# Thirty-eight products that nobody reads, in the attention's tail and the first score step of a one-core decoder block

## The chip, the cores and the metric

The kernel runs on one core of a Trainium2 chip. The metric is the device time of one execution in microseconds. Three executions of the kernel before took 869.7, 869.7 and 870.72 us; the median is 869.7 us. Lower is better.

## The reference

The block has three sublayers on x of 8 batches, 128 tokens and 256 features, each with a layer norm ahead and a residual add behind:

```
x = x + delta_rule_attention(layernorm(x))   # 16 heads, state 128 x 256 a head, causal convolutions
x = x + cross_attention(layernorm(x), ctx)   # 16 heads of 8 features, 256 rows against 256
x = x + experts(layernorm(x))                # shared + 8 experts, two of them weighted in
```

The cross attention treats the 256 features of a batch as 256 rows of 128 tokens. For each batch and head it computes

```
dot  = einsum('bhdt,bhds->bhts', q, k) / sqrt(8)
amap = softmax(mask * dot - (1 - mask) * 1e6) * mask
out  = einsum('bhts,bhds->bhdt', amap, v)
```

## The kernel before, in words

Each engine has its instructions written out in order by hand, and semaphores tie the engines together. PE's stream (the kernel's last long function) has these parts.

First come 32 steps of the delta-rule attention (STEPS = 32: 16 heads in two halves of four batches). Their pieces, such as `proj_`, `grams`, `c_t1`, `y0`, `y1` and `outp`, are interleaved. Behind the last full step comes a tail in which the pieces of the last steps, `s30` to `s32`, stand among the projections of the cross attention: `k_proj` (keys, L2210 and L2211), `v_proj` (values, L2222) and `q_proj` (queries, L2233 and L2234). `outp` (L2079) makes the last sublayer output, which DVE adds to x (L1479). DVE then takes the moments of the new x (L1345, L1348) and normalizes it (L1354).

Then PE has a row of waits on semaphores, for everything of the attention, and goes on to the cross attention. It has 64 units: a unit is two heads' 256 x 256 scores of one batch, so that a batch has 8. For unit n `top_scores(n)` (L2352) makes the scores in PSUM, DVE takes their maxima (L1693), and POOL splits the negative maxima of four units into two f16 parts (L755, L757, L759: `mrow`). `turn_max` (L2364) transposes these onto the query stack's rows and DVE adds them (L1685), so that `energies(n)` (L2377) makes scores with the maximum already taken off. ACT takes the exponential (L1193, `et`), and `values` (L2394) multiplies by the values into the bank `avb`. `swap_den` (L2404) exchanges halves of the denominators once a batch. DVE's L1616 stacks a query projection's high and low parts; ACT's L1129 makes the high part.

`batch_step(w)` is one of eight steps over the batches. It holds eight `top_scores`, eight `energies` (six units behind), the `values` of up to four pairs, two `turn_max` and up to four halves of `q_proj`, in a fixed order. Scores and energies share three pairs of PSUM banks in rotation, so that `top_scores(3)` waits for the first maximum. Step 0 has no `values` and only two `energies` at its end. Behind the eight steps come the rest of the cross attention and the experts.

`t.matmul(out, stationary, moving)` is the form of a product. `ident16` is a 128 x 128 identity in f16, `kst` the stacked keys in f16, and `avb` is bank 6 of PSUM, which holds nothing that is still needed at the places of the change.

Of the kernel before, what the change touches and what calls it, by code (L numbers as in the profile page):

```python
# [105 lines left out]
def need(eng, sem, value):  # L106

    if isinstance(value, int) and value <= 0:
        return
    eng.wait_ge(sem, value)  # L110
# [13 lines left out]
def build(nc, d, out):  # L124
    with ExitStack() as whole:
# [3 lines left out]
        def sb(name, shape, dt, ctx=whole):  # L129
            return ctx.enter_context(nc.sbuf_tensor(name, shape, dt))  # L130
# [10 lines left out]
        ident16 = sb("ident16", [P, P], F16)  # L141
# [16 lines left out]
        kst = sb("kst", [P, B, 4, H], F16)  # L158
# [184 lines left out]
        avb, misc = psum[:, 6, :], psum[:, 7, :]  # L343
# [12 lines left out]
        def pair_of(kind, n):  # L356
            return pairs[place[kind, n] % 3]
# [1495 lines left out]
        def _(pe):  # L1853
            t = nc.tensor
# [342 lines left out]
            def k_proj(bb, hh):  # L2197

                pe.wait_ge(ctx_masked, bb + 1)
                if bb == 0:  # L2200
                    pe.wait_ge(mask_ready, 1)
                    pe.wait_ge(bias_ready, 1)
                    pe.wait_ge(z_sb[hh], STEPS - 1)
                elif bb == NK:
                    pe.wait_ge(z_sb[hh], STEPS)
                else:
                    pe.wait_ge(k_stack[hh], bb)
                for g2 in range(2):
                    o = ubank[hh][:, g2 * H:(g2 + 1) * H]
                    t.matmul(o, wks[:, 2 * hh + g2], ctxs[:, bb], start=True, stop=False)  # L2210
                    mm = t.matmul(o, bias5[:, 1, 2 * hh + g2], mask5[:, bb], start=False, stop=True)  # L2211
                mm.then_inc(k_psum[hh], 1)

            def v_proj(i):
# [7 lines left out]
                    mm = t.matmul(ebank[i % 2][:, n * P:(n + 1) * P], ctxs[:, 2 * i + n // 2, n % 2 * P:(n % 2 + 1) * P], wvt[:], start=True, stop=True)  # L2222
                mm.then_inc(v_psum[i % 2], 1)

            def q_proj(h, g2):
                b, hh = h // 2, h % 2
                if g2 == 0:
                    pe.wait_ge(x_masked, b + 1)
                    need(pe, q_stack, h)
                    if h >= 3:  # L2230
                        pe.wait_ge(q_full, h - 2)
                o = misc[:, g2 * H:(g2 + 1) * H]
                t.matmul(o, wqs[:, 2 * hh + g2], xm[:, b], start=True, stop=False)  # L2233
                mm = t.matmul(o, bias5[0:4, 0, 2 * hh + g2], mask5[0:4, b], start=False, stop=True)  # L2234
                if g2 == 1:
                    mm.then_inc(q_psum, 1)
# [75 lines left out]
            k_proj(6, 1)  # L2312
            pe.wait_ge(added, STEPS * 2 - 2)
            q_proj(0, 0)
            q_proj(0, 1)
            k_proj(7, 0)
            s32.y1()
            k_proj(7, 1)
            q_proj(1, 0)
            q_proj(1, 1)  # L2320
            s32.outp(0)
            s32.outp(1)


            pe.wait_ge(z_sb[0], STEPS)
# [11 lines left out]
            def pair_free(kind, n):  # L2337
                user = freed(kind, n)
                if user is not None:
                    pe.wait_ge(max_done if user[0] == "max" else e_done, user[1] + 1)  # L2340

            def top_scores(n):
                if not 0 <= n < UNITS:
                    return
                h, g2, rp = n // 4, n // 2 % 2, n % 2
                b, gq = h // 2, h % 2 * 2 + g2
                pe.wait_ge(q_stack, h + 1)
                pair_free("max", n)
                for tt in range(2):
                    for rr in range(2):  # L2350
                        ps = slice(32 * (2 * rp + rr), 32 * (2 * rp + rr) + 32)
                        mm = t.matmul(pair_of("max", n)[:, rr, tt * H:(tt + 1) * H], qst[ps, h % 4, g2, tt * P:(tt + 1) * P], kst[ps, b, gq, :], start=True, stop=True)  # L2352
                mm.then_inc(max_psum, 1)

            def turn_max(h):
                if not 0 <= h < 2 * B:
                    return
                pe.wait_ge(max_split, 3 * h + 3)
                need(pe, q_stack, min(h + 3, 2 * B))
                need(pe, q_full, h)  # L2360
                for g2 in range(2):
                    for tt in range(2):
                        o = g2 * H + tt * P
                        mm = t.transpose(misc.bitcast(F16)[:, o:o + P], mrow[:, h % 2, tt, g2].rearrange("p r n -> p (r n)"), ident16[:])  # L2364
                mm.then_inc(row_psum, 1)

            def energies(n):
                if not 0 <= n < UNITS:
                    return
                h, g2, rp = n // 4, n // 2 % 2, n % 2  # L2370
                b, gq = h // 2, h % 2 * 2 + g2
                pe.wait_ge(q_full, h + 1)
                pair_free("exp", n)
                for st in range(2):
                    for rr in range(2):
                        ps = slice(32 * (2 * rp + rr), 32 * (2 * rp + rr) + 32)
                        mm = t.matmul(pair_of("exp", n)[:, rr, st * H:(st + 1) * H], kst[ps, b, gq, st * P:(st + 1) * P], qst[ps, h % 4, g2, :], start=True, stop=True)  # L2377
                mm.then_inc(e_psum, 1)

            def values(gn, st):  # L2380
                if not 0 <= gn < 4 * B:
                    return
                b, gq = gn // 4, gn % 4
                if st == 0:
                    pe.wait_ge(e_done, 2 * gn + 2)
                    if gq == 0:
                        pe.wait_ge(v_wide, 2 * b + 2)
                        need(pe, den_ln, b)
                        if b == 0:
                            pe.wait_ge(late_set, 4)  # L2390
                half_ = gq // 2 * H
                for r in range(4):
                    ps = slice(32 * r, 32 * r + 32)
                    mm = t.matmul(avb[ps, half_:half_ + H], vz[:, b % 2, st, r, 32 * gq:32 * gq + 32], et[:, gn % 4, r, st],  # L2394
                                  start=(gq == 0 and st == 0), stop=(gq % 2 == 1 and st == 1), skip_group_check=True)
                if st == 1:
                    mm.then_inc(o_psum, 1)

            def swap_den(b):
                if not 0 <= b < B:  # L2400
                    return
                pe.wait_ge(den_sb, b + 1)
                pe.wait_ge(num_sb, b + 1)
                t.matmul(avb[:, 0:H], swap[:], den[:], start=True, stop=True).then_inc(swap_psum, 1)  # L2404

            def batch_step(w):
                values(4 * w - 5, 0)
                top_scores(8 * w)
                values(4 * w - 5, 1)
                energies(8 * w - 6)  # L2410
                turn_max(2 * w - 1)
                top_scores(8 * w + 1)
                energies(8 * w - 5)
                if 2 <= 2 * w + 2 < 2 * B:
                    q_proj(2 * w + 2, 0)
                top_scores(8 * w + 2)
                swap_den(w - 2)
                if 2 <= 2 * w + 2 < 2 * B:
                    q_proj(2 * w + 2, 1)
                energies(8 * w - 4)  # L2420
                top_scores(8 * w + 3)
                values(4 * w - 4, 0)
                energies(8 * w - 3)
                values(4 * w - 4, 1)
                top_scores(8 * w + 4)
                values(4 * w - 3, 0)
                energies(8 * w - 2)
                values(4 * w - 3, 1)
                turn_max(2 * w)
                top_scores(8 * w + 5)  # L2430
                energies(8 * w - 1)
                values(4 * w - 2, 0)
                top_scores(8 * w + 6)
                if 2 <= 2 * w + 3 < 2 * B:
                    q_proj(2 * w + 3, 0)
                energies(8 * w)
                top_scores(8 * w + 7)
                if 2 <= 2 * w + 3 < 2 * B:
                    q_proj(2 * w + 3, 1)
                values(4 * w - 2, 1)  # L2440
                energies(8 * w + 1)

            for w in range(B):
                batch_step(w)
# [230 lines left out]
```

## Time and profile before

| | |
|---|---|
| median of three runs | 869.7 us (869.7 to 870.72) |
| the profiled execution | 870.83 us, span 869.0 us |
| PE busy, share of the span | 804.5 us, 93% |
| DVE, ACT, POOL busy | 712.8, 657.7, 619.0 us |
| mean granted TensorE clock | 0.963 |
| chain that ended last | PE 84%, POOL 4%, DVE 4% |

The span is the time from the first to the last instruction; the execution's own time is 1.8 us longer. The page's second part cuts the span into 40 slices of 21.7 us. The digit of an engine is its busy share in tenths, and PEclk is the TensorE clock that was granted, in tenths of full speed; slice 32 begins at 673.5 us. In the table by stretches the columns are start and end, length, and for each engine the busy time with the number of instructions, then the granted clock, the share of DMA and GB/s. In a timeline a row is: start, time from the first start to the last end, engine, line, operation, tiles, shapes and count, and in brackets the idle time before it with what ended it. PE's products overlap, so that the distance between two starts is the price of one, and the duration is longer.

### The profile page before, as it was taken

What the parts mean: (1) busy time and instruction counts of PE and PEld (TensorE: products, weight loads), DVE (VectorE), ACT (ScalarE), POOL (GpSimd) and SP (SyncE); (2) the same over time, 40 slices, a digit from 0 to 9 for tenths busy, and PEclk for the clock granted to TensorE, in tenths of its full rate; (3) what the DMA queues carried; (4) which work ended last, traced back from release to release, by engine and by line L of the source; (5) the groups of instructions that cost most, each with busy time, mean ns of one, the idle gap of its engine ahead of it and who ended that gap; (6) DMA issues with size and microseconds to landing.
All of it is one profiled execution on the core that took longest, in us unless ns stands there. A gap on an engine that the chain in (4) does not pass through costs nothing.

```text
span 869.0 us, 22776 instructions
## 1 busy us (share of the span) xinstructions
PE 804.5 (93%) x7798; PEld 551.9 (64%) x7834; DVE 712.8 (82%) x1202; ACT 657.7 (76%) x1036; POOL 619.0 (71%) x749
## 2 busy tenths in 40 slices
PE   3589999999999999999999999999999699999987
PEld 2257777777777777777777777777775233433554
DVE  6788888898888888888889888899677858996634
ACT  3688888888888888888888888888733347876633
POOL 4879979898898988989898898986650214342248
PEclk9999999999999999999999999999999559995999
DMA  8301000000100001000000100000000700000051
GB/s 225 114 2 38 25 14 26 14 26 12 36 24 12 24 12 36 15 21 24 12 24 12 36 24 12 0 1 2 2 2 0 122 6 2 2 2 1 2 134 49
DMA packets 32032, 24.94 MB, mean 29 GB/s; under 512 B 3310, under 2 KB 29614, under 8 KB 31851
## 3 DMA queue, kind: packets, MB, share of 16 engines
q1 hardware_dynamic: 29227, 19.75, 8.1%
q0 software_dynamic: 2752, 4.49, 2.5%
q8 instruction: 33, 0.54, 0.3%
q14 instruction: 20, 0.16, 0.1%
HBM read 25.85 MB, written 1.06 MB: 31 GB/s over the span
## 4 chain that ended last, share of the span: by engine, by line
PE 84%; POOL 4%; DVE 4%; issue 3%; ACT 2%; DMA 1%; SPq 1%; POOLq 0%; DVEq 0%; ACTq 0%
PE psum L1904 18%; PE psum L1975 7%; PE psum L2079 6%; PE psum L2394 4%; PE psum L2047 4%; PE psum L2058 3%; PE psum L2003 3%; PE psum L1922 3%; PE psum L1921 3%; PE psum L1920 3%; PE psum L2233 2%; PE psum L1996 2%; PE psum L1962 2%; PE psum L2006 2%; PE psum L2210 2%
## 5 line engine op out<-in xcount | busy, mean ns | idle before, releaser
L1461 DVE SCALAR_TENSOR_TENSOR y<-psum,cwh,y 128x508 f32<-128x508 f32 (+2 forms) x384 | 281.9, 741 | 11.1 <-ACT y L938 2.1
L558 POOL TENSOR_TENSOR ct<-lm,levels 128x256 f16<-128x256 f32 x224 | 151.0, 704 | 8.1 <-DVE lm L1472 8.1
L544 POOL TENSOR_TENSOR sql<-sq,sqh 128x1024 f16<-128x1024 f32 x32 | 68.4, 2137 | 58.7 <-ACT sqh L995 38.8
L938 ACT ACTIVATE y<-psum,cwh 128x512 f32<-128x512 f32 x128 | 99.2, 775 | 3.2 <-PE psum L1904 3.1
L1193 ACT ACTIVATE et<-psum 128x1024 f32<-128x1024 f32 x64 | 64.6, 1023 | 34.2 <-PE psum L2377 34.1
L1904 PE MATMUL psum<-xth,whi 128*128 128x512 f16 x256 | 77.0, 383 | 10.7 <-DVE y L1461 7.9
L1693 DVE TENSOR_REDUCE mx<-psum 128x4 f32<-128x1024 f32 x64 | 75.8, 1218 | 13.4 <-PE psum L2352 13.1
L1904 PE MATMUL psum<-xth,wlo 128*128 128x512 f16 x256 | 77.1, 383 | 0.0
L1904 PE MATMUL psum<-xtl,whi 128*128 128x512 f16 x256 | 77.0, 383 | 0.0
L1429 DVE TENSOR_TENSOR ux<-ux,psum 128x512 f16<-128x512 f16 x96 | 65.8, 686 | 6.6 <-PE psum L2006 6.0
L1975 PE MATMUL psum<-kq 128*128 128x256 f32 x256 | 70.0, 397 | 0.0
L1920 PE MATMUL psum<-woh,vth 128*128 128x256 f16 x256 | 69.8, 273 | 0.0
L1921 PE MATMUL psum<-wol,vth 128*128 128x256 f16 x256 | 69.8, 273 | 0.0
L1922 PE MATMUL psum<-woh,vtl 128*128 128x256 f16 x256 | 69.8, 273 | 0.0
L755 POOL TENSOR_SCALAR mxs<-mx 128x16 f32<-128x16 f32 x16 | 4.0, 252 | 90.9 <-DVE mx L1693 90.9
L531 POOL TENSOR_TENSOR vtl<-vt,vth 128x1024 f16<-128x1024 f32 x32 | 68.4, 2138 | 0.1
L931 ACT ACTIVATE zz<-psum 128x512 f32<-128x512 f32 x64 | 38.2, 597 | 35.2 <-PE psum L1922 35.1
L2079 PE MATMUL psum<-zz,pt 128*128 128x256 f32 x256 | 63.1, 389 | 0.0
L2003 PE MATMUL psum<-t1z,ux 128*128 128x64 f16 x768 | 54.1, 193 | 8.7 <-ACT t1z L922 8.7
L525 POOL TENSOR_TENSOR vth<-vt,zero 128x1024 f16<-128x1024 f32 x32 | 60.6, 1894 | 0.0
L1996 PEld LDWEIGHTS psum<-ux,ct 128*128 128x128 f16 x768 | 42.7, 98 | 24.5 <-DVE ux L1429 2.6
L2003 PEld LDWEIGHTS psum<-t1z,ux 128*128 128x128 f16 x768 | 40.3, 97 | 24.6 <-ACT t1z L922 12.1
(239 smaller groups left out, 2293.3 us busy)
## 6 DMA issues: line engine op xcount, KB each, us to landing
wraw<-in_L_attn_Wv SPq DMA_DIRECT2D x32, 128.0 KB, 2.4
wo<-in_L_attn_Wo SPq DMA_DIRECT2D x16, 256.0 KB, 2.8
wraw<-in_L_attn_Wk SPq DMA_DIRECT2D x16, 128.0 KB, 2.2
wraw<-in_L_attn_Wq SPq DMA_DIRECT2D x16, 128.0 KB, 2.3
x<-in_x SPq DMA_DIRECT2D x8, 128.0 KB, 3.8
maskrow<-in_mask_row POOLq DMA_DIRECT2D x1, 1024.0 KB, 5.0
ctxs<-in_ctx SPq DMA_DIRECT2D x1, 1024.0 KB, 7.1
wide<-comb_mem SPq DMA_DIRECT2D x4, 256.0 KB, 5.1
```

Source lines behind the costliest of these rows:

```text
L531: g.tensor_tensor(lo, f, hi, ALU.subtract).then_inc(v_split, 1)
L558: g.tensor_tensor(dst, src, pick.unsqueeze(1).to_broadcast([P, NB, T // (2 * m), m]), ALU.mult).then_inc(masked[l], 1)
L938: s.activation(y[:, n], ubank[n % 2].rearrange("p (j t) -> p j t", j=NB), ACT.Identity, scale=cwh[:, (a.c // 2) % 2, n, TAPS - 1:TAPS], bi ...
L1461: v.scalar_tensor_tensor(out=y[:, n, :, sh:], in0=u[:, :, 0:T - sh], scalar=cwh[:, (a.c // 2) % 2, n, TAPS - 1 - sh:TAPS - sh], in1=y[:, n ...
L1693: v.tensor_reduce(mx[:, h % 2, g2, 2 * rp:2 * rp + 2].rearrange("p r a -> p (r a)"), pair_of("max", n).rearrange("p r (a s) -> p (r a) s", ...
L1904: mm = t.matmul(ubank[n % 2], w_[:, hr, n, ch, :], x_[:, ch, cols], start=(m == 0), stop=(m == len(ops) - 1))
L1920: t.matmul(o, vth[:, r, vc, toks], woh[:, hr, vc, :], start=(vc == 0), stop=False)
L1921: t.matmul(o, vth[:, r, vc, toks], wol[:, hr, vc, :], start=False, stop=False)
L1922: mm = t.matmul(o, vtl[:, r, vc, toks], woh[:, hr, vc, :], start=False, stop=(vc == 1))
L1975: mm = t.matmul(ebank[hf][:, jj * 256:(jj + 1) * 256], kq[:, r, j, 0, :], kq[:, r, j].rearrange("p a t -> p (a t)"), start=True, stop=True)
L2003: mm = t.matmul(half(dst[:, 256 + j * 64:256 + (j + 1) * 64], m), turned(st.c % 2, 0, j), first_half(t1z[:, level - 1, j * T:(j + 1) * T], ...
L2079: mm = t.matmul(c_banks(c)[hf][:, jj * H:(jj + 1) * H], pt[:, j], zz[:, c.c % 2, j], start=True, stop=True)
```

## The change

A new function `keep_busy(n)` makes n products of the identity with 512 columns of the key stack into `avb`. No semaphore is raised by them and none is waited for, and no engine reads what they write; the first `values` begins the bank anew. Fourteen stand in the tail: 3, 2, 2 and 3 between `q_proj(0, 1)` and `q_proj(1, 0)`, and 4 behind the last `outp`, ahead of the row of waits. Twenty-four stand in step 0 of the cross attention, three behind each of its eight `top_scores`. Nothing else differs: the opening of the two kernels is the same.

```diff
+            def keep_busy(n):
+                for _ in range(n):
+                    t.matmul(avb, ident16[:], kst[:, 0, 0:2].rearrange("p g n -> p (g n)"), start=True, stop=True)
+
             pe.wait_ge(added, STEPS * 2 - 2)
             q_proj(0, 0)
             q_proj(0, 1)
+            keep_busy(3)
             k_proj(7, 0)
+            keep_busy(2)
             s32.y1()
+            keep_busy(2)
             k_proj(7, 1)
+            keep_busy(3)
             q_proj(1, 0)
             q_proj(1, 1)
             s32.outp(0)
             s32.outp(1)
+            keep_busy(4)
...
             def batch_step(w):
                 values(4 * w - 5, 0)
                 top_scores(8 * w)
+                if w == 0:
+                    keep_busy(3)
                 values(4 * w - 5, 1)
                 energies(8 * w - 6)
                 turn_max(2 * w - 1)
                 top_scores(8 * w + 1)
+                if w == 0:
+                    keep_busy(3)
...
```

The same two lines stand behind the other six `top_scores` of the step.

PE's order from the last key projection to the first scores, before (L2210 and L2211 keys, L2233 and L2234 queries, L2079 `outp`, L2352 scores):

```order
L2210 MATMUL psum<-ctxs,wks 128x256
L2211 MATMUL psum<-mask,bias 128x256
L2233 MATMUL psum<-xm,wqs 128x256
L2234 MATMUL psum<-mask,bias 128x256
L2233 MATMUL psum<-xm,wqs 128x256
L2234 MATMUL psum<-mask,bias 128x256
L2079 MATMUL psum<-zz,pt 128x256 x4
L2352 MATMUL psum<-kst,qst 128x256 x8
```

The same place now (L2227 is `keep_busy`, L2237 and L2238 the queries, L2361 the scores):

```order
L2210 MATMUL psum<-ctxs,wks 128x256
L2211 MATMUL psum<-mask,bias 128x256
L2227 MATMUL psum<-kst,ident 128x512 x3
L2237 MATMUL psum<-xm,wqs 128x256
L2238 MATMUL psum<-mask,bias 128x256
L2237 MATMUL psum<-xm,wqs 128x256
L2238 MATMUL psum<-mask,bias 128x256
L2079 MATMUL psum<-zz,pt 128x256 x4
L2227 MATMUL psum<-kst,ident 128x512 x4
L2361 MATMUL psum<-kst,qst 128x256 x4
L2227 MATMUL psum<-kst,ident 128x512 x3
```

Three products now stand ahead of the last query projection and so ahead of `outp`, four behind it, and the first two units' scores are apart.

PE's order around the first `turn_max` (L2364), before: the scores of units 3 and 4, the transposes, the scores of units 5 and 6, half a projection, the first energies (L2377) and the scores of unit 7:

```order
L2352 MATMUL psum<-kst,qst 128x256 x8
L2364 MATMUL psum<-ident,mrow 128x128 x4
L2352 MATMUL psum<-kst,qst 128x256 x8
L2233 MATMUL psum<-xm,wqs 128x256
L2234 MATMUL psum<-mask,bias 128x256
L2377 MATMUL psum<-qst,kst 128x256 x4
L2352 MATMUL psum<-kst,qst 128x256 x4
```

The same place now, from the scores of unit 4 (L2373 the transposes, L2386 the energies):

```order
L2361 MATMUL psum<-kst,qst 128x256 x4
L2227 MATMUL psum<-kst,ident 128x512 x3
L2373 MATMUL psum<-ident,mrow 128x128 x4
L2361 MATMUL psum<-kst,qst 128x256 x4
L2227 MATMUL psum<-kst,ident 128x512 x3
L2361 MATMUL psum<-kst,qst 128x256 x4
L2227 MATMUL psum<-kst,ident 128x512 x3
L2237 MATMUL psum<-xm,wqs 128x256
L2238 MATMUL psum<-mask,bias 128x256
L2386 MATMUL psum<-qst,kst 128x256 x4
L2361 MATMUL psum<-kst,qst 128x256 x4
L2227 MATMUL psum<-kst,ident 128x512 x3
```

Three products stand ahead of the transposes, and six between them and the projection and energies that follow.

## Rows read from the trace of the kernel before

**Rows 1.** The page's slices: the granted clock.

```profile
PEclk9999999999999999999999999999999559995999
```

**Rows 2.** Busy time by stretch: tail, first step, half clock, a full step, the end.

```profile
660.00:670.00 10.00, 10.00 (x55) 5.89 (x53) 7.30 (x15) 3.56 (x7) 1.58 (x2) 1.00 0.00 0
670.00:690.00 20.00, 12.68 (x84) 5.95 (x83) 17.65 (x28) 5.14 (x8) 4.74 (x10) 0.69 0.43 80
700.00:710.00 10.00, 10.00 (x70) 3.37 (x70) 4.96 (x6) 4.03 (x5) 1.42 (x4) 0.50 0.00 0
728.60:741.80 13.20, 13.17 (x151) 5.40 (x151) 12.18 (x15) 10.37 (x15) 5.22 (x13) 1.00 0.01 2
784.00:804.00 20.00, 19.75 (x164) 6.54 (x162) 12.98 (x27) 12.46 (x17) 5.76 (x14) 0.50 0.00 1
```

**Rows 3.** The same by single microseconds, where the clock falls, rises and falls.

```profile
677.00:678.00 1.00, 0.00 (x0) 0.00 (x0) 1.00 (x2) 0.22 (x1) 0.00 (x0) 0.88 0.41 122
...
718.00:719.00 1.00, 1.00 (x16) 0.23 (x12) 1.00 (x2) 0.98 (x2) 0.03 (x1) 0.64 0.00 0
...
783.00:784.00 1.00, 0.81 (x9) 0.29 (x8) 1.00 (x2) 0.66 (x2) 0.00 (x0) 0.78 0.00 0
```

**Rows 4.** Timeline of PE, from the last output product to the first transposes.

```profile
670.78 1.99 PE L2079 MATMUL psum<-zz,pt 128*128 128x256 f32 x8
674.28 0.41 PE L2352 MATMUL psum<-kst,qst 32*128 32x256 f16 x8 [1.51 <-DVE x L1479]
674.62 0.70 PE L2233 MATMUL psum<-xm,wqs 128*128 128x256 f32 x2
...
675.68 0.70 PE L2233 MATMUL psum<-xm,wqs 128*128 128x256 f32 x2
...
678.48 0.61 PE L2352 MATMUL psum<-kst,qst 32*128 32x256 f16 x4 [1.89 <-DVE mx L1693]
...
682.89 0.61 PE L2364 MATMUL psum<-ident,mrow 128*128 128x128 f16 x4 [2.67 <-POOL mrow L759]
```

**Rows 5.** Timeline of DVE in the same stretch.

```profile
672.18 1.32 DVE L1479 TENSOR_TENSOR x<-x,psum 128x512 f32<-128x512 f32 x2
...
677.12 4.61 DVE L1693 TENSOR_REDUCE mx<-psum 128x4 f32<-128x1024 f32 x4
...
684.08 3.49 DVE L1693 TENSOR_REDUCE mx<-psum 128x4 f32<-128x1024 f32 x3
```

**Rows 6.** Timeline of PE: first query projections of steps 1 to 4, and one swap.

```profile
690.77 1.22 PE L2233 MATMUL psum<-xm,wqs 128*128 128x256 f32 x2
...
712.83 1.22 PE L2233 MATMUL psum<-xm,wqs 128*128 128x256 f32 x2
...
728.60 0.67 PE L2233 MATMUL psum<-xm,wqs 128*128 128x256 f32 x2
...
729.63 0.70 PE L2404 MATMUL psum<-den,swap 128*128 128x256 f32 x2
730.16 0.59 PE L2233 MATMUL psum<-xm,wqs 128*128 128x256 f32 x2
...
741.79 0.67 PE L2233 MATMUL psum<-xm,wqs 128*128 128x256 f32 x2
```

**Rows 7.** Timeline of PE in the opening: L1904, products of 512 columns.

```profile
25.44 0.59 PE L1904 MATMUL psum<-xth,whi 128*128 128x512 f16 x2 [1.08 <-DVE y L1461]
25.87 0.59 PE L1904 MATMUL psum<-xtl,whi 128*128 128x512 f16 x2
...
29.66 1.01 PE L1904 MATMUL psum<-xth,whi 128*128 128x512 f16 x2 [2.77 <-DVE y L1461]
30.47 1.06 PE L1904 MATMUL psum<-xtl,whi 128*128 128x512 f16 x2
...
32.89 0.59 PE L1904 MATMUL psum<-xth,whi 128*128 128x512 f16 x2 [0.52 <-POOL wlo L502]
...
37.64 0.59 PE L1904 MATMUL psum<-xth,whi 128*128 128x512 f16 x2 [1.96 <-DVE y L1461]
```

More of the change, by code:

```diff
@@ L2416, in batch_step @@
                 top_scores(8 * w + 2)
+                if w == 0:
+                    keep_busy(3)
                 swap_den(w - 2)
@@ L2421, in batch_step @@
                 top_scores(8 * w + 3)
+                if w == 0:
+                    keep_busy(3)
                 values(4 * w - 4, 0)
@@ L2425, in batch_step @@
                 top_scores(8 * w + 4)
+                if w == 0:
+                    keep_busy(3)
                 values(4 * w - 3, 0)
@@ L2430, in batch_step @@
                 top_scores(8 * w + 5)
+                if w == 0:
+                    keep_busy(3)
                 energies(8 * w - 1)
@@ L2433, in batch_step @@
                 top_scores(8 * w + 6)
+                if w == 0:
+                    keep_busy(3)
                 if 2 <= 2 * w + 3 < 2 * B:
@@ L2437, in batch_step @@
                 top_scores(8 * w + 7)
+                if w == 0:
+                    keep_busy(3)
                 if 2 <= 2 * w + 3 < 2 * B:
```

## The prediction, made before the run

> **What bounds the kernel now.** I read the page's slices first. The row PEclk holds 9 except in slices 32, 33 and 37 of 40, where it is 5 [rows 1]. The table by stretches says what that is worth: PE is 10.00 of 10 us busy in the attention's tail at clock 1.00, then loses a third of 670 to 690 us, and from 700 to 710 us it is 10.00 of 10 us busy again at 0.50, which is 1.2 of 2.4 GHz [rows 2]. The fine stretches place the edges: the clock falls at 677.9 us (0.88 in that microsecond), comes back at 718.6 and falls again at 783.8 [rows 3]. So in the cross attention there are 40.8 us at half clock behind the first fall and about 20 us behind the second.
>
> The timeline of PE shows what it did before the first fall. Behind the last output product (670.78, ends at 672.8) it stood 1.51 us for x, made twelve score products of 32 rows and two query projections, then stood 1.89 us for a maximum and 2.67 us for the first split of the maxima [rows 4]. DVE's timeline says why: from 672.2 to 687.6 us it adds x, normalizes and takes eight maxima, four of them in 4.61 us, 1.15 each [rows 5], and in 670 to 690 us it is busy for 17.65 of 20 [rows 2]. So the first step of the cross attention is bound by DVE, and there half a clock costs little. What follows is bound by PE. The first projection of step 1 stands at 690.77, of step 2 at 712.83, of step 3 at 728.60, of step 4 at 741.79 [rows 6]: one step takes 22.06 us at half clock and 13.19 us at full clock, with PE 13.17 of 13.20 us busy and DVE 12.18 [rows 2].
>
> **The ten products in the tail.** A product of `keep_busy` reads 128x512 of f16 and has 128 stationary columns, as L1904's. The page's mean of 383 ns is latency; the price is the distance: two from 25.44 to 25.87 at full clock, 0.215 us each, and two from 29.66 to 30.47 at half clock, 0.41 us each, where I take twice the first, 0.43 [rows 7]. The second piece of order shows ten of them between `q_proj(0, 1)` and the last `outp` (3 + 2 + 2 + 3). PE has no idle time there [rows 2], its semaphores were all up before, and DVE's second add of x starts at 672.84, 0.07 us behind the product that it reads (672.18 plus one of two adds of 0.66; L2079 ends at 672.77) [rows 4, 5]. Nothing hides them: 10 x 0.215 = 2.15 us later for x, the normalization, the maxima and all that follows.
>
> **The four behind the last output product.** 0.86 us, ahead of the wait for x. PE waits 1.51 us there [rows 4], and x comes 2.15 us later together with PE. The cover is that wait; cost 0. Without it they would cost at most 0.86 us.
>
> **The 24 in step 0.** Three are 0.65 us at full clock. DVE's maxima are the cover. In times of the new kernel (before + 2.15): the first score products stand at 676.4. A projection half with a score unit behind it takes 1.06 us (674.62 to 675.68), a unit alone 0.17 to 0.25 (two in the 0.34 ahead of 674.62) [rows 4]. The fifth unit must wait for the second maximum, 677.12 + 2.30 + 2.15 = 681.6 [rows 5], and with its unit and three fillers PE is through at 682.7. The transposes of L2364 wait for the fourth maximum and POOL's three steps; they stood at 682.89 [rows 4] and come at about 685.05. Behind them, at full clock: the transposes 0.3 (0.61 at half clock), two units and two sets 0.25 + 0.65 each, energies 0.25, a projection half with the eighth unit 1.06, so that this unit ends at 688.5. DVE wants it at 684.08 + 2 x 1.16 + 2.15 = 688.55 [rows 5]. So it is just in time, with nothing to spare; the next projection is behind three more products and its query stack comes some 0.4 us late on DVE, of which I let 0.2 reach the path. Both ends: 0, if step 1's first projection waits for a maximum anyway, and 9 x 0.43 = 3.9 us, if the nine behind the transposes run at half clock, where what ended in time no longer does.
>
> **What the clock gives back.** If PE stays at 2.4 GHz from 677.9 on: step 1 from projection to projection takes 13.19 less the 0.54 of the swap product that it has not yet (L2404 at 729.63, the next product at 730.16, [rows 6]) = 12.65 instead of 22.06, saved 9.4. DVE's 12.18 in a step leaves room [rows 2, 6]. Step 2 takes 13.19 instead of 15.77, saved 2.6. In step 0 I take nothing, since DVE bounds it. Sum: 12.0 saved, 2.15 + 0.2 paid: 9.65 us less. The profiled execution took 870.83 us, so 861.2 us; the median of the runs shown is 1.1 us lower, and I take 860.5 us.
>
> Does it stay? The opening has the same kind of product and shows both outcomes. It fell in an idle stretch of 2.77 us (29.66: a pair lasts 1.01 us), was up again behind six products (32.89: 0.59 us), and held across an idle stretch of 1.96 us (37.64: 0.59 us) [rows 7]. In the tail the longest idle stretch of the new kernel is 682.7 to 685.05, 2.35 us, with fifteen fillers close ahead of it and six close behind: between the two rows, nearer to 1.96. The second doubtful place is the start of step 1, 690 to 693 us, where no filler stands, PE makes mostly products of 32 rows, and the transposes and energies wait for the ninth maximum. Two projection halves are what fills it. I hold both for slightly more likely passed than not.
>
> A rule speaks about this. The Trainium skill, "TensorE: Matmul & The Clock Gate", section "Why this matters for your kernels", says to keep TensorE continuously busy in order to get the full clock. The trace does not bear it out as busy time alone: in 700 to 710 us PE is 10.00 of 10 us busy and the clock is 0.50 throughout [rows 2]. By the rule a fall would be made good soon after 690 us; by the row it lasts until step 2, in both kernels. This matters for the third rival only, which the rule would make as cheap as the second.
>
> **Rivals.**
> 1. *The clock also holds in the last step.* It fell at 783.8 with PE still 0.81 busy in that microsecond [rows 3], at a place that the change leaves alone. That is a much thinner pause than the first one's, so it is near the edge, and with the work 9.6 us earlier it may pass. Then 784 to 804 us, 20 us of PE at 0.50, shrinks: PE's work by 12.65/22.06 to 11.5 us, but DVE has 12.98 and ACT 12.46 there [rows 2] and they wait for one another, so some 14 us. Gain 6 us more: 855 us. Against it: that nothing there is changed.
> 2. *The clock falls in step 0 or early in step 1 and is brought back soon.* For it: the opening's products raised it [rows 7], and nine fillers follow the first doubtful idle stretch. A few microseconds at half clock, of which each costs 1 - 0.573 = 0.43 where PE bounds, and part of the 3.9 us: 863 to 867 us.
> 3. *Slower: the clock falls behind the last filler.* Place: start of step 1, 691 to 695 us. From there the kernel is the old one, at half clock until step 2 as in 690 to 718 us [rows 2, 3], 2.15 + 0.2 us later: 870.83 + 2.35 = 873.2, against the median 872. If it falls already ahead of the transposes and is not brought back, the nine products at half clock add up to 3.9: 876. For it: the products of 32 rows never raised the clock in 28 us of a fully busy PE. It decides from where more than 9.65/0.43 = 22 of the 28 us remain at half clock.
> 4. *The products do not count or count little, and the tail has slack for them that I do not see*: within 0.2% of before. For it only that gains and prices can cancel.
>
> **Chances.** Forecast (860.5, itself 858.5 to 862.5): 0.31. Rival 1 (855): 0.19. Rival 2 (865): 0.13. Rival 3 (872 to 876): 0.30. Rival 4: 0.07. Faster by over 0.2%, which is 1.7 us and about what a measurement of this kernel can tell: 0.63; within: 0.07; slower: 0.30. The range goes from rival 1's 853.5 to 873.5, and leaves out the dearer half of rival 3.
>
> **What would show it.** Right: PEclk 9 in slices 32 and 33; L2079's last group near 672.9; L2364's first near 685.0, four transposes well under the 0.61 us of half clock; first projections of steps 1, 2 and 3 near 693.1, 705.8 and 719.1; ten more products in the tail and no more idle time of DVE in 674 to 690. Wrong: a 5 in those slices; a distance of 0.43 between fillers; DVE idle between the sixth and the eighth maximum, which would mean that the fillers themselves hold up step 0. If x is added less than 2 us later, the tail had slack. Slice 37 tells the forecast from rival 1.

## The result, and the profile after

| | before | after |
|---|---|---|
| profiled execution | 870.83 us, span 869.0 | 860.98 us, span 859.2 |
| executions compared | 869.7 to 870.84 us | 860.98 and 861.88 us |
| mean granted clock | 0.963 | 0.980 |
| PE busy | 804.5 us | 806.5 us |

The ratio of these executions is 0.9899, with a 95% interval of 0.9875 to 0.9923: 1.0% faster. The forecast was 860.5 us. Two further executions of the changed kernel took 876.4 and 881.3 us at lower mean clocks (0.963 and 0.959) and are not in the ratio; their median with the two above is 869.15 us.

The page's row of the granted clock, which answers to [rows 1]:

```profile
PEclk9699999999999999999999999999999989997999
```

Slices 32 and 33, at 5 before, are gone; one slice in the same place now has 8, and the last stretch at half clock costs one 7. The 6 in the second slice is the opening, which is chance: the same instructions stand there. The stretches of [rows 2], in the trace after:

```profile
660.00:670.00 10.00, 10.00 (x58) 6.19 (x57) 7.42 (x14) 3.47 (x8) 1.59 (x2) 1.00 0.01 2
670.00:690.00 20.00, 17.22 (x86) 7.66 (x85) 14.98 (x25) 2.30 (x5) 3.32 (x6) 0.88 0.29 55
700.00:710.00 10.00, 9.98 (x117) 4.04 (x114) 8.88 (x12) 7.42 (x10) 3.46 (x9) 1.00 0.01 2
728.60:741.80 13.20, 13.17 (x156) 5.40 (x150) 12.18 (x15) 10.37 (x14) 5.22 (x14) 1.00 0.01 3
784.00:804.00 20.00, 17.48 (x189) 8.46 (x186) 15.09 (x35) 15.89 (x33) 7.85 (x13) 0.91 0.01 2
```

PE is busy for 4.5 us more in 670 to 690 us, and 700 to 710 us runs at 1.00 and holds 117 products' records instead of 70. But the clock is 0.88 in 670 to 690 us, so it did fall. The fine stretches, as in [rows 3]:

```profile
685.00:686.00 1.00, 0.76 (x8) 0.48 (x8) 0.98 (x2) 0.00 (x0) 1.00 (x3) 0.58 0.00 0
691.00:692.00 1.00, 1.00 (x7) 0.28 (x3) 0.59 (x1) 0.65 (x1) 0.00 (x0) 0.51 1.10 214
...
777.00:778.00 1.00, 1.00 (x16) 0.16 (x8) 1.00 (x2) 0.83 (x1) 0.00 (x0) 0.66 0.00 0
787.00:788.00 1.00, 1.00 (x14) 0.33 (x14) 1.00 (x2) 0.56 (x2) 0.00 (x0) 0.72 0.00 0
```

The clock falls at 685.2 and is back at 692.0 us, 6.8 us instead of 41.0; it falls again at 777.3 and is back at 787.6 us, 10.2 us instead of 20.5. (The clock has two levels here, so 0.58 in a microsecond means 0.84 us of it at half. Read so, [rows 3] put the edges of before at 677.8, 718.7 and 783.6 us, up to 0.2 us from where the prediction has them, and the first stretch at 41.0 us, not 40.8.) PE's timeline says what it did before each edge (L2227 is `keep_busy`, L2373 the transposes, L2361 the scores):

```profile
673.12 1.99 PE L2079 MATMUL psum<-zz,pt 128*128 128x256 f32 x8
674.95 1.03 PE L2227 MATMUL psum<-kst,ident 128*128 128x512 f16 x4
676.62 0.39 PE L2361 MATMUL psum<-kst,qst 32*128 32x256 f16 x4 [0.64 <-issue]
...
682.28 0.82 PE L2227 MATMUL psum<-kst,ident 128*128 128x512 f16 x3
685.24 0.61 PE L2373 MATMUL psum<-ident,mrow 128*128 128x128 f16 x4 [2.13 <-POOL mrow L759]
685.78 0.60 PE L2361 MATMUL psum<-kst,qst 32*128 32x256 f16 x4
686.32 1.46 PE L2227 MATMUL psum<-kst,ident 128*128 128x512 f16 x3
687.71 0.61 PE L2361 MATMUL psum<-kst,qst 32*128 32x256 f16 x4
688.25 1.46 PE L2227 MATMUL psum<-kst,ident 128*128 128x512 f16 x3
...
691.24 1.17 PE L2227 MATMUL psum<-kst,ident 128*128 128x512 f16 x3
```

Before, the clock fell in the wait for the first maximum, 1.89 us long [rows 4]; fillers stand there now, and the clock stays up. It falls at the end of the next idle stretch, the one ahead of the transposes, 2.13 us long (2.67 before, [rows 4]). The fillers behind it run at half clock, three from 686.32 to the scores at 687.71 (1.46 us for three instead of 0.82), and the clock is back during the last three. What the slow fillers did to DVE, against [rows 5]:

```profile
674.52 1.32 DVE L1479 TENSOR_TENSOR x<-x,psum 128x512 f32<-128x512 f32 x2
...
679.46 4.61 DVE L1693 TENSOR_REDUCE mx<-psum 128x4 f32<-128x1024 f32 x4
...
686.43 1.23 DVE L1693 TENSOR_REDUCE mx<-psum 128x4 f32<-128x1024 f32 x1
688.35 1.22 DVE L1693 TENSOR_REDUCE mx<-psum 128x4 f32<-128x1024 f32 x1 [0.70 <-PE psum L2361]
691.41 1.23 DVE L1693 TENSOR_REDUCE mx<-psum 128x4 f32<-128x1024 f32 x1 [1.84 <-PE psum L2361]
```

The sixth, seventh and eighth maximum were one block of 3.49 us before; now DVE waits 0.70 and 1.84 us for scores that stand behind three fillers each. The first projections of steps 1, 2 and 3, as in [rows 6]:

```profile
696.07 0.69 PE L2237 MATMUL psum<-xm,wqs 128*128 128x256 f32 x2
...
708.86 0.67 PE L2237 MATMUL psum<-xm,wqs 128*128 128x256 f32 x2
...
722.05 0.67 PE L2237 MATMUL psum<-xm,wqs 128*128 128x256 f32 x2
```

Step 1 begins 5.3 us later than before and takes 12.79 us instead of 22.06; step 2 takes 13.19 instead of 15.77; step 3 begins 6.55 us earlier. The other 3.1 us of the gain come in the last step. The first transposes of the experts' features, before and after:

```profile
805.79 0.63 PE L2453 MATMUL psum<-ident,xn 128*128 128x128 f32 x4 [0.21 <-ACT et L1193]
...
796.14 0.63 PE L2478 MATMUL psum<-ident,xn 128*128 128x128 f32 x4 [0.84 <-ACT et L1193]
```

They stand 9.65 us earlier.

### The profile page after: what moved, and what is told of

Same layout as the page of the kernel before. It is cut to its first block, busy times and chain, and to the rows that moved or that the text cites. A ratio compares the mean times of both kernels' runs of the same rounds, so it can differ in the third digit from the quotient of the medians.

```text
span 859.2 us, 22888 instructions
## 1 busy us (share of the span) xinstructions
PE 806.5 (94%) x7872; PEld 552.2 (64%) x7872; DVE 712.5 (83%) x1202; ACT 657.6 (77%) x1036; POOL 619.0 (72%) x749
## 4 chain that ended last, share of the span: by engine, by line
PE 86%; DVE 4%; POOL 4%; ACT 2%; issue 2%; SPq 1%; DMA 0%; POOLq 0%; DVEq 0%
PE psum L1904 18%; PE psum L1975 7%; PE psum L2079 7%; PE psum L2047 4%; PE psum L2403 4%; PE psum L2058 4%; PE psum L2003 3%; PE psum L1922 3%; PE psum L1921 3%; PE psum L1920 3%; PE psum L1996 2%; PE psum L1959 2%; PE psum L2006 2%; PE psum L2522 2%; PE psum L2210 2%; PE psum L2237 2%
## 5 line engine op out<-in xcount | busy, mean ns | idle before, releaser
L1904 PE MATMUL psum<-xth,whi 128*128 128x512 f16 x256 | 78.3, 388 | 10.4 <-DVE y L1461 6.2
L1904 PE MATMUL psum<-xtl,whi 128*128 128x512 f16 x256 | 78.4, 388 | 0.0
L1904 PE MATMUL psum<-xth,wlo 128*128 128x512 f16 x256 | 78.0, 387 | 0.0
L2079 PE MATMUL psum<-zz,pt 128*128 128x256 f32 x256 | 63.1, 389 | 0.0
```

The lines of the kernel that those rows point to most:

```text
L1904: mm = t.matmul(ubank[n % 2], w_[:, hr, n, ch, :], x_[:, ch, cols], start=(m == 0), stop=(m == len(ops) - 1))
L2079: mm = t.matmul(c_banks(c)[hf][:, jj * H:(jj + 1) * H], pt[:, j], zz[:, c.c % 2, j], start=True, stop=True)
```

## The experiments

Medians are over all executions of a kernel; the ratio, with its 95% interval, compares as above with the kernel before, which ran beside each. "Comes back" and "falls" are read from the profiled execution.

**e1: the ten products of the tail alone.**

```diff
             s32.outp(1)
-            keep_busy(4)
...
-                if w == 0:
-                    keep_busy(3)
```

> Only the ten products between q_proj(0, 1) and q_proj(1, 0) are kept; the four behind the last outp and the 24 of step 0 are gone. Theory (the tail has no idle time, and the gain of the change comes from the clock in the cross attention alone): x is added 10 x 0.215 = 2.15 us later, the clock falls where it fell before, and the time is 2.0 to 2.3 us above the kernel before, 872 to 873 us. Rival A (the tail has slack for them): within 0.5 us of before. Rival B (the ten alone keep the clock up behind them): PEclk 1.00 in 678 to 690 us and 862 us or less.

Median 875.89 us (862.66 to 885.95), profiled 867.23; ratio 0.994 (0.9877 to 1.0003). None of the seven executions lies at the 872 to 873 us of the theory: three are below 868 and four above 875. The time alone does not decide. The trace gives the price without the clock in it: both ends of the tail, at full clock (first row `q_proj(0, 0)`, second `outp`).

```profile
664.63 0.70 PE L2237 MATMUL psum<-xm,wqs 128*128 128x256 f32 x2
...
673.46 1.99 PE L2079 MATMUL psum<-zz,pt 128*128 128x256 f32 x8
```

The distance is 8.83 us, as in the change (664.29 to 673.12), and 6.91 before (663.87 to 670.78). So the ten cost 1.92 us, and rival A, slack in the tail, falls. The clock fell at 678.2 and came back at 719.2 us as before, so rival B falls too. The execution is still 3.6 us below that of before, since in its last step the clock did not fall at all. Nothing in that step was changed, so it varies as the opening does, and it hides the 1.92.

**e2: the same 38 products with 32 rows instead of 128.**

```diff
-                    t.matmul(avb, ident16[:], kst[:, 0, 0:2].rearrange("p g n -> p (g n)"), start=True, stop=True)
+                    t.matmul(avb, ident16[0:32, :], kst[0:32, 0, 0:2].rearrange("p g n -> p (g n)"), start=True, stop=True)
```

> All 38 products as in the change, but each with 32 of the 128 rows (the first 32 of the identity and of the keys), so that PE is busy for as long with a quarter of the array's rows. Theory (busy time alone does not hold or raise the clock, full products do): the distance stays 0.215 us, the clock falls in 675 to 686 us and is not brought back in step 0; it stays at 0.50 until step 2 or 3, and the kernel is slower than before by the 2.15 us of the ten and up to 3.9 us of the nine at half clock: 873 to 877 us. Rival (what counts is that PE is busy at all): the time of the change, 861 us, with at most 7 us at half clock in 670 to 700 us.

Median 874.85 us (873.13 to 884.05), ratio 1.008 (1.0038 to 1.0121): slower, as the theory had it. The page's clock, and two stretches of it:

```profile
PEclk9999999999999999999999999999999558998999
```

```profile
670.00:690.00 20.00, 19.45 (x84) 8.20 (x83) 15.07 (x25) 2.29 (x5) 3.33 (x6) 0.68 0.28 56
...
700.00:710.00 10.00, 10.00 (x79) 2.98 (x79) 5.35 (x7) 4.58 (x5) 2.28 (x6) 0.50 0.00 0
```

PE is busy for 19.45 of 20 us, more than in the change (17.22), and the clock falls at 677.3 and stays at 0.50 until 725.1 us. So busy time does not hold the clock here: with 128 rows the same fillers carried it past 677 us to 685.2, and brought it back in 6.8 us. By the rule of the Trainium skill to keep TensorE busy ("TensorE: Matmul & The Clock Gate", "Why this matters for your kernels") e2 should have held as well as the change; the measurement decides against it. One part of the theory failed: the ten cost more than in the change, as `outp` stands 9.31 us behind the first projection (663.19 to 672.50) and not 8.83, so 2.40 us for ten.

**e3: the change with its idle stretches covered.**

```diff
+                if w == 1:
+                    keep_busy(4)
                 turn_max(2 * w - 1)
                 top_scores(8 * w + 1)
                 if w == 0:
                     keep_busy(3)
+                if w == 1:
+                    keep_busy(2)
...
+                if w == 0:
+                    keep_busy(9)
                 turn_max(2 * w)
```

> The change, and more of its products where its PE stands idle at the doubtful places: nine more ahead of the first turn_max (1.94 of the 2.13 us idle there), and in step 1 four ahead of its first turn_max and two behind top_scores(9). Theory (the fall at 685 us comes from that idle stretch, and its price is the few microseconds at half clock with nine fillers in them): the clock stays 1.00 from 670 to 770 us, L2361's ninth score product and with it step 1 come 2 to 2.5 us earlier than in the change, and the time is 857.5 to 859.5 us. Rival (the added products delay the transposes, or DVE bounds there anyway and the short fall costs nothing): 861 to 863 us.

Median 857.72 us (855.46 to 860.55), ratio 0.9848 (0.9805 to 0.9891). PE's timeline:

```profile
682.24 2.76 PE L2227 MATMUL psum<-kst,ident 128*128 128x512 f16 x12
685.21 0.40 PE L2373 MATMUL psum<-ident,mrow 128*128 128x128 f16 x4 [0.20 <-POOL mrow L759]
...
693.04 0.69 PE L2237 MATMUL psum<-xm,wqs 128*128 128x256 f32 x2
...
705.82 0.67 PE L2237 MATMUL psum<-xm,wqs 128*128 128x256 f32 x2
...
719.02 0.67 PE L2237 MATMUL psum<-xm,wqs 128*128 128x256 f32 x2
```

The idle stretch is 0.20 us, the transposes come no later than in the change (685.24), and the clock is 1.00 from 43.2 to 773.7 us. Step 1 begins at 693.04, 3.03 us ahead of the change. So the fall of 6.8 us cost 3.0 us, and without it the three steps stand where the prediction put them: 693.1, 705.8 and 719.1. The profiled execution took 860.55 us, the longest of the four, as the clock fell for 13.7 us in its last step and for 3.4 us behind it.

**e4: e3 without the ten.**

```diff
             q_proj(0, 1)
-            keep_busy(3)
             k_proj(7, 0)
-            keep_busy(2)
             s32.y1()
-            keep_busy(2)
             k_proj(7, 1)
-            keep_busy(3)
             q_proj(1, 0)
```

> As the kernel with the covered places, without the ten products of the tail. Theory (the ten stand on the path and do nothing for the clock, since the tail holds it without them in the kernel before until 677.9 us): 2.15 us below the covered kernel, 855.5 to 857.5 us, with the clock at 1.00 as there. Rival (the ten are needed for the clock to pass the waits behind the tail): it falls in 675 to 690 us and the time is 860 us or more.

Median 853.79 us (852.61 to 854.77), ratio 0.9815 (0.9779 to 0.985): below e3 and 1.7 us below the range of its theory, and with e7 the fastest kernel of the study. The page's clock, and the tail as in e1:

```profile
PEclk9999999999999999999999999999999999999999
```

```profile
663.37 0.70 PE L2237 MATMUL psum<-xm,wqs 128*128 128x256 f32 x2
...
670.28 1.99 PE L2079 MATMUL psum<-zz,pt 128*128 128x256 f32 x8
```

The distance is 6.91 us again, 1.92 less, and the clock holds without the ten. Of the 3.9 us between the medians of e3 and e4 the ten are half. In the profiled pair 0.9 us more come from the opening (the tail begins at 663.37 instead of 673.08 - 8.83 = 664.25), and the rest from a last fall of 3.4 us in e4 (at 782.7) against 13.7 and 3.4 in e3.

**e5: the change without the ten.** The edit is e4's.

> The change without its ten products ahead of outp; the four behind outp and the 24 of step 0 stay. From the distance between q_proj(0, 0) and L2079 with and without the ten (8.83 and 6.91 us) they cost 1.92 us. Theory (they do nothing else): L2079 near 670.3, and where the idle stretch ahead of the first transposes lets the clock fall, it is brought back as in the change; 859 us, 2 us below the change's 861. Rival (the ten help the clock behind them to stay up or come back): it stays at 0.50 beyond 700 us and the kernel is at 870 us or above.

Median 859.74 us (853.29 to 877.18), profiled 857.94, ratio 0.9922 (0.9861 to 0.9982). The clock fell at 685.8 us and was back after 3.4 us. `outp` is 6.90 us behind the first projection (at 672.00, as the opening was late by a microsecond). The theory was right, and nothing shows the ten to help the clock. The place of the fall asks for a second look (L2369 the transposes, L2357 the scores):

```profile
684.12 0.40 PE L2369 MATMUL psum<-ident,mrow 128*128 128x128 f16 x4 [2.14 <-POOL mrow L759]
684.45 0.39 PE L2357 MATMUL psum<-kst,qst 32*128 32x256 f16 x4
684.77 0.82 PE L2227 MATMUL psum<-kst,ident 128*128 128x512 f16 x3
```

The idle stretch ends at 684.12, so the clock fell 1.7 us behind it, with transposes, scores and three fillers already through at full clock. From `outp` to the first projection of step 1 it is 21.51 us (672.00 to 693.51), against 22.95 in the change and 19.95 or 19.96 in the profiles without a fall there (e3, e4, e6). So a fall of 3.4 us costs 1.6 us and one of 6.8 us costs 3.0. And a fall there is not certain: the execution of 853.29 us has a mean granted clock of 0.998, which leaves about 3.4 us at half clock in all of it (twice 0.002 of 851.5 us); every profile of the study has at least that much within its first 48 us.

**e6 and e9: which cover matters.** e6 has e4's nine products ahead of the first `turn_max` and not the six of step 1; e9 the six and not the nine.

> As e4, but of the added covers only the nine products ahead of the first turn_max; the six of step 1 are gone. Theory (the idle stretch of 2.13 us ahead of the transposes is what lets the clock fall, the start of step 1 holds by its projections): as e4, 852.6 to 855 us. Rival (the thin start of step 1 with idle 1.08 and 0.47 us is a second place of the fall, and nothing stands behind it that brings the clock back): it falls between 690 and 697 us and stays at 0.50 for 10 us or more, 860 to 872 us.

> As e4 with the six products of step 1 and without the nine ahead of the first turn_max: the fourth corner beside e5 (neither), e6 (the nine alone) and e4 (both). Theory (the start of step 1 is the place from which the clock does not come back; the fall ahead of the first transposes is mended by the nine products behind them): executions between 854 and 862 us, none above 865, since a fall in the idle stretch costs some 3 to 4 us and no more. Rival (a fall ahead of the transposes can also stay): executions at 870 us or above.

e6: median 864.96 us (855.92 to 894.98), ratio 0.9981 (0.9931 to 1.0032), no gain. Its profiled execution, the fastest, had no fall there, and `outp` to step 1 took 19.95 us. e9: median 856.99 us (853.56 to 859.86), ratio 0.9855 (0.9798 to 0.9912); profiled, the clock fell at 685.1 and was back after 3.4 us, at 858.13 us. e9's theory came out but for the lowest execution, 0.4 us under its range. Both medians go against e6's theory and with its rival: the start of step 1 needs its own fillers more than the stretch ahead of the transposes does. The likely reason is that behind the latter nine fillers follow and behind the former none. The longer executions of e6 did run longer at half clock: twice what the mean clock lacks, times the span, makes about 22 us in the profiled execution (0.987), 34 us at 864.12 us (0.980) and 114 us at 894.98 us (0.936). That their clock fell at 690 to 697 us is argued from this pair; no trace of such an execution was taken, and the old stretch behind that place is 28 us long, so in the longest it must have been down elsewhere too. Why e6's median lies even above that of e5, which has neither cover, is open.

**e7 and e8: the last step and the opening covered as well.** e7 adds to e4 three products ahead of `top_scores(58)`, with a wait of PE's added in front of them, one behind `energies(52)` (not in the extract) and two ahead of the last `turn_max`. `keep_misc` is `keep_busy` into bank 7 of PSUM. e8 adds to e7 eight, six and five products in the opening; `keep_open` multiplies the transposed x by itself.

```diff
+                if w == 7:
+                    pe.wait_ge(q_full, 14)
+                    keep_misc(3)
...
             energies(58)
+            keep_misc(2)
             turn_max(15)
```

```diff
             m2.proj_(2)
+            keep_open(8)
             m1.proj_(1)
+            keep_open(6)
             m1.proj_(0)
             gate_cumulate()
             m1.norms()
+            keep_open(5)
```

> As e4, with six products more in the last step and behind it (three ahead of top_scores(58), one behind energies(52), two ahead of the last turn_max), in the bank misc, where PE waited for ACT and DVE. Theory (the second fall, at 773 to 784 us, comes from those waits, and at half clock PE is behind ACT and DVE there): the clock stays 1.00 to the end of the cross attention; up to 1.5 us below e4, 851 to 853 us. Rival (ACT and DVE bound that stretch in any case, or the products delay the energies): 853 to 855 us as e4.

> As e7, with 19 products more in the opening (8, 6 and 5, of the transposed x by itself) where PE waits 2.6, 1.9 and 1.7 us for DVE and POOL. Theory (the opening's fall at 28 to 30 us costs 0.4 to 0.9 us, as the start of the tail is 663.87 us after a short fall and 664.29 us after a long one): the clock stays 1.00 from 19 us on and the time is 0.5 to 1 us below e7. Rival (they delay the projections and so DVE, which bounds the opening): 1 to 3 us above e7.

e7: median 853.77 us (853.01 to 856.05); e8: 854.2 us (853.76 to 856.34). Both are as e4's 853.79 (measured on another chip), so neither theory got its gain. In e7 the clock held until 802.2 us, past the whole cross attention. From `outp` to the first features it took 116.91 us, against 117.52 in e4, which fell for 3.4 us there, and 116.49 in e6, which did not fall there and has none of these six. So they won 0.6 us over e4's trace and cost 0.4 themselves; PE still waits 0.85 us for ACT ahead of the first features. In e8 the clock held until 44.2 us and then fell for 3.4 us, and the tail began at 664.41 us, no earlier than with the fall (663.37 in e4). Covering the opening moved its fall and gained nothing that the traces show.

**e10: the changed kernel again.**

> The changed kernel itself once more, on the chip and in the rounds of e9. Theory: about 861 us, 1 to 2 us above e5's 859, as the ten products cost 1.92 us. Rival (the ten make it steadier, so that they earn their price): its executions lie at or below e5's.

Profiled 861.33 us, the lowest 859.84 and the median 868.82 (to 879.39), with no ratio. Its trace repeats the first one's: idle 2.14 us ahead of the transposes, a fall at 685.3 and back at 692.1. Its median lies above e5's, so the rival, that the ten earn their price, has nothing for it. With the first four these are eight executions of the changed kernel: four between 859.8 and 861.9 us, four between 876.3 and 881.3, and none between. The gain of 1.0% holds for the lower half only. The median of the eight is 869.1 us, against 870.2 for the first four of the kernel before and 871.8 for the nine that ran beside e10, so over all executions the change as it stands is not shown to be faster.

## Why the prediction was right, and where it was not

The total came out (861.2 worked out for the profiled execution, 860.98 measured), but by luck: two misses of 3 us cancel. The gain in steps 1 and 2 is the part that was right in mechanism and size. In the prediction's terms what happened is rival 2, which alone would have made 864 us; the last step then gave 3.1 us that the forecast had not counted. Two of its own signs of being wrong came: fillers some 0.43 us apart, and DVE idle between its sixth and eighth maximum.

- *The ten products.* Forecast 2.15 us, measured 1.92 (e1, e4). The price of one held (0.65 us for three); but in three places the pair of products right behind a filler takes 0.53 us to the next product and not 0.63, which gives back the difference of 0.2.
- *The four, and the fillers ahead of the transposes, at 0.* Right. The first scores are 0.64 us behind the end of the four, and the transposes come at 685.24, forecast 685.05: 0.42 us later for the opening and 0.23 earlier for the ten.
- *"I hold both for slightly more likely passed than not."* This step failed. The idle stretch, forecast at 2.35 us and 2.13 in the trace, let the clock fall, at its end or up to 1.8 us behind it, in all four profiles with fillers close ahead of it (the change, e5, e9, e10) and in none with the stretch covered (e3, e4, e6, e7, e8). One execution without a trace, of e5, can hardly have fallen there. The comparison with the opening, where the clock outlived 1.96 us, was too weak for an even bet.
- *The price of that fall.* Rival 2 had the mechanism: brought back by the fillers behind it. It cost 3.0 us (696.07 in the change, 693.04 in e3), within the bound of 3.9, and through the place named: six fillers at half clock and three while it came back, and DVE idle between its sixth and eighth maximum. Per microsecond at half clock that is 0.44 us, and 0.46 in e5, where the prediction had 0.43.
- *The 12.0 us saved in steps 1 and 2.* Right. Step 1 was forecast at 12.65 us and took 12.79, step 2 at 13.19 and took 13.19. Together 11.9.
- *The last step, forecast unchanged.* It gave 3.1 us, half of rival 1: the clock fell in the same place, for 10.2 us and not 20.5. How long it stays down there varies from kernel to kernel (3.4 us in e4, 13.7 in e3), and in e1 it did not fall. From the first projection of step 3 to the first features it took 77.19 us before, 74.09 in the change and 70.58 in e1, so the whole fall is worth 6.6 us, close to rival 1's 6: a third of a microsecond for each at half clock, less than the 0.43 of the steps that PE bounds.
- *Rival 3.* Its weak place, the start of step 1, is where e6 and e9 part. The 876.4 and 881.3 us of the two other executions lie at and above its upper figure. Their mean clocks (0.963, 0.959) make about 65 and 72 us at half clock against 34 in the profiled execution, so 30 and 38 us more, where the old stretch at the start of step 1 is 28 us. That fits rival 3, but no trace of them was taken, so the place is not shown.
- *From 861.2 to 860.5.* The prediction says that its median is 1.1 us lower than the profiled execution and then takes off 0.7; it gives no reason.

In sum: 11.9 saved, 1.9 and 3.0 paid, 0.4 to the opening, and 3.1 back in the last step make 9.7 of the 9.85 us measured.

## What to carry to other kernels

Where PE goes from dense work to a stretch in which it waits for another engine, price the next PE-bound stretch at half clock, and fill the waits themselves, up to the moment of the release (e3: 12 products in 2.76 us, transposes no later). Do not put fillers where PE is already busy: the ten cost 1.9 us and no run shows a use of them. How few of the other 28 would do is not shown, as no run takes them out one group at a time. Put them also where a fall would not be mended by later dense work, as at the start of step 1: covering the idle stretch alone (e6) gained nothing in the median. Let a filler use all rows of the array. And take several executions of a kernel whose clock is near such a fall: one profile shows only one of the ways it can go.

## What the runs showed of the hardware that was not expected

Products that read 32 rows kept PE busy for 19.45 of 20 us and the clock still fell, and stayed at half for 47.8 us (e2); the same count of 128-row products brought it back in 6.8 us. A fall can come behind an idle stretch and not in it: 1.7 us in e5 and 1.8 in e9, with PE at work again. The kernel before, whose four first executions agreed within 1.2 us, spread from 858 to 897 us over the later sessions. The kernels with the six products in step 1 (e3, e4, e7, e8, e9; 20 executions) all lay between 852.6 and 860.6 us; of the 28 of the kernels with 128-row fillers in step 0 and without these six (the change, e5, e6, e10) nine took over 870. What a microsecond at half clock costs is 0.44 to 0.46 us at the start of the cross attention and 0.3 at its end, where PE waits for ACT and DVE.
